# State recurrence of the last attention: how the C rows reach all partitions

## The chip, the cores and the metric

The kernel runs on 1 core of a Trainium2 chip. The metric is the device time of one execution, in microseconds (us), as the median of several runs. Its engines are TensorE (PE in the profile, its weight loads PEld), VectorE (DVE), ScalarE (ACT), GpSimd (POOL) and SyncE (SP), which here only issues DMAs.

## The reference

A decoder of four layers, three sublayers each, on 16 sequences of 128 tokens and 256 features in fp32. What the change touches is the first sublayer of the last layer, a selective state space recurrence (Mamba) with 512 inner channels and 16 states:

```python
dbc = jnp.einsum('bld,ed->ble', x_in, x_proj_w)
delta_in, Bp, Cp = dbc[..., :512], dbc[..., 512:528], dbc[..., 528:]
delta = jax.nn.softplus(jnp.einsum('bld,ed->ble', delta_in, dt_proj_w) + dt_proj_b)
def step(h, inp):
    dt, bt, ct, xt = inp
    dA = jnp.exp(dt[:, :, None] * A[None])
    h = dA * h + dt[:, :, None] * bt[:, None, :] * xt[:, :, None]
    y = jnp.einsum('bds,bs->bd', h, ct) + D * xt
    return (h, y)
```

For each of 16 states there is a value of B and one of C for every token, and each multiplies all 512 channels.

## The kernel before, in words

The last attention is `l3_attn`. Tokens lie along the free dimension, channels on the partitions. The 16 sequences go in 4 groups of 4, so a tile is 128 channels x 512 tokens, and a group has 4 such channel tiles. A **unit** is one state of one pair of channel tiles: 32 units a group (`UNITS`; states 0 to 15 for the first pair of tiles, then again for the second), 128 in all, counted by `n`. A unit goes through the engines in this order:

- TensorE `spread_b` (L2749) spreads row `s` of B over the 128 partitions: a matmul of a 96-row one-hot column with the three bf16 parts of B and C (`bc`). It runs two units ahead in two PSUM banks, and waits until DVE has used the row of two units before.
- DVE (L3013) multiplies it by step times input into a slot of `ring`; ScalarE `decay` (L2912) makes exp(step x A) of both tiles in PSUM; DVE runs two scans (L3019).
- GpSimd (L3097) multiplies the state by the **C row** `s` in `c_row`, a tile of 16 rows that all partitions hold in SBUF.
- TensorE `add_up` (L2766) adds the product to the sums of the two tiles in PSUM, by an fp32 matmul with the identity (four matmul records a unit).

After each half group (16 units) `gate_sums` on DVE (L2996) takes the sums out of PSUM; at unit 1 of a group it takes those of the last half of the group before, and so waits for the last `add_up` of it.

**How C rows come about before the change.** `spread_c` on TensorE spreads a row of C like one of B, into one of two side banks, and `take_c` on ScalarE (L2886) copies it from there to `c_row`. There are 64 of each: 6 before the loop (`EARLY_C`), then one beside unit `n` where `c_row_of(n)` says so: units 0 to 9 of group 0, units 18 to 31 of groups 0 to 2 (rows 0 to 13 of the next group), and units 0 and 1 of groups 1 to 3 (rows 14 and 15).

**What sets the order.** Each engine has one written-out order. In step `n` TensorE does `spread_b(n + 2)`, `spread_c`, `add_up(n - 1)`, then `beside(n)`, the side work of the other groups (projections, convolution L2717, turning L2744). The C rows and the side work share the two side banks in turn:

```python
n = number[name] = len(number)
if n >= 2:
    pe.wait_ge(taken, n - 1)
return net.banks[SIDE[n % 2]]
```

So whatever asks for a side bank waits until ScalarE has emptied it of the work two before. ScalarE does in step `n` `decay(n)`, then, at unit 1 of a group, `silu_z` (L2899) and `silu_u` (L2895), each with a load of its function table, then `take_side(n - 3)` and `take_c` of row `n - 2`; then comes `decay(n + 1)`, with another table load after a silu. `logarithm` (L2891) and `root` (L2903) come at units 18 and 21.

The three bf16 parts of B and C are made once a group: `take_bc` on ScalarE copies the projection from PSUM to `bc` and, in fp32, to `bc_rest[0]` (L2846, L2847); GpSimd `rest` (L3077) subtracts, twice, the second time over `bc_rest[0]`; ScalarE `middle_part` and `low_part` (L2851 to L2857) round. Only then may rows be spread. SP's block is `prefetch`, one DMA of the next sublayer's inputs.

Of the kernel before, what the change touches and what calls it, by code (L numbers as in the profile page):

```python
# [5 lines left out]
F32 = mybir.dt.float32  # L6
# [7 lines left out]
P = 128  # L14
# [2566 lines left out]
    return None  # L2581


EARLY_C = 6


def c_row_of(u):


    g, n = divmod(u, UNITS)  # L2590
    if g == 0 and n + EARLY_C < STATES:
        return 0, n + EARLY_C
    if n >= 18 and g + 1 < GROUPS:
        return g + 1, n - 18
    if n < 2 and g >= 1:
        return g, STATES - 2 + n
    return None


class StepWeights:  # L2600


# [33 lines left out]
def l3_attn(net, prefetch):  # L2636
# [10 lines left out]
    with ExitStack() as sub:  # L2647
# [20 lines left out]
        (filled, taken, part_ready, rest_ready, a_ready, tables_ready, u_ready, z_ready,  # L2668
         bc_ready, ex_ready, lost_ready, positive_ready, log_ready, dt_ready, dtu_ready, b_in_psum, drive_ready,
         decay_ready, state_ready, out_ready, summed, y_taken, yz_ready, r_ready, var_ready, rstd_ready, x_ready,  # L2670
         dve_steps, act_steps) = net.signals(29)
        number = {}
        rows_ = 2 * STATES

# [11 lines left out]
        def normalise(engine, wait, g, b):  # L2686
            wait(rstd_ready, g + 1)
            engine.tensor_scalar(x_of(g)[:, b, :], net.r[:, b, :], net.mv[:, b, 0:1], net.rstd[:, b:b + 1],
                                 ALU.subtract, ALU.mult).then_inc(x_ready, 1)

        with nc.Block() as block:
            @block.sync
            def _(sp):
                prefetch(sp)

            @block.tensor
            def _(pe):
                pe.wait_ge(net.ready["l3_attn"], 16)
# [50 lines left out]
                    return pe.matmul(out[:], pick[:, col:col + 1].broadcast_to([PARTS, P]), bc[g % 2][:],  # L2749
                                     start=True, stop=True)  # L2750

                def spread_c(g, s):
                    spread_out(side("c", g, s), g, STATES + s).then_inc(filled, 1)

                def spread_b(n):
                    if n >= 2:
                        pe.wait_ge(drive_ready, n - 1)
# [36 lines left out]
                for m in range(DT_):  # L2794
                    step_project(0, m)
                pe.wait_ge(tables_ready, 1)
                for s in range(EARLY_C):
                    spread_c(0, s)
                for n in range(2):
                    spread_b(n)  # L2800
                for m in range(DT_):
# [1 line left out]
                for n in range(total):  # L2803
                    if n + 2 < total:
                        spread_b(n + 2)
                    if c_row_of(n):
                        spread_c(*c_row_of(n))
                    if n:
                        add_up(n - 1)
                    beside(n)  # L2810
# [7 lines left out]
            def _(act):  # L2818
# [3 lines left out]
                def bank(*name):  # L2822
                    n = number[name]
                    act.wait_ge(filled, n + 1)
                    return net.banks[SIDE[n % 2]]
# [54 lines left out]
                def take_turned(g, f):  # L2880
                    nc.scalar.copy(net.xT_all[:, g, f, :], bank("turn", g, f)[:]).then_inc(taken, 1)

                def take_c(g, s):
                    if g:
                        act.wait_ge(out_ready, (g - 1) * UNITS + STATES + s + 1)
                    nc.scalar.copy(c_row[:, s, :], bank("c", g, s)[:]).then_inc(taken, 1)  # L2886

                def logarithm(g):
                    act.wait_ge(ex_ready, DT_ * (g + 1))
                    act.wait_ge(lost_ready, DT_ * (g + 1))  # L2890
# [55 lines left out]
                low_part(0)  # L2946
                take_step(0, 2)
                take_step(0, 3)
                for s in range(EARLY_C):
                    take_c(0, s)  # L2950
                logarithm(0)
                act.wait_ge(a_ready, 1)
                act.wait_ge(tables_ready, 1)
                for n in range(total):
                    g, at = divmod(n, UNITS)
                    decay(n)
                    if n < 2:
                        take_conv(1, 2 * n)
                        take_conv(1, 2 * n + 1)
                    if at == 1:  # L2960
                        if g >= 1:
                            silu_z(g - 1)
                        if g + 1 < GROUPS:
                            silu_u(g + 1)
                    if n >= 3:
                        take_side(n - 3)
                    if n >= 2 and c_row_of(n - 2):
                        take_c(*c_row_of(n - 2))
                    if at == 9 and g + 1 < GROUPS:
                        middle_part(g + 1)  # L2970
                    if at == 12 and g + 1 < GROUPS:
                        low_part(g + 1)
                    if at == 18 and g + 1 < GROUPS:
                        logarithm(g + 1)
                    if at == 21 and g >= 1:
                        root(g - 1)
                    if n == total - 2:
                        silu_z(GROUPS - 1)
# [66 lines left out]
            @block.gpsimd  # L3045
            def _(pool):
                tt = nc.gpsimd.tensor_tensor

                def lost_part(g, m):

                    pool.wait_ge(ex_ready, DT_ * g + m + 1)
                    tt(one_ex[m % 2], one_ex[m % 2], ex[:, m, :], ALU.subtract).then_inc(lost_ready, 1)

                def positive_part(g, m):
                    pool.wait_ge(lost_ready, DT_ * g + m + 1)
                    tt(positive[:, m, :], positive[:, m, :], one_ex[m % 2], ALU.subtract).then_inc(positive_ready, 1)

                def step(g, m):
                    pool.wait_ge(log_ready, g + 1)
                    pool.wait_ge(positive_ready, DT_ * g + m + 1)  # L3060
                    if g:
                        pool.wait_ge(decay_ready, 2 * ((g - 1) * UNITS + STATES * (m // 2 + 1)))
                    tt(dt[:, m, :], ex[:, m, :], positive[:, m, :], ALU.add).then_inc(dt_ready, 1)

                def step_times_input(g, m):
                    pool.wait_ge(dt_ready, DT_ * g + m + 1)
                    if g:
                        pool.wait_ge(drive_ready, (g - 1) * UNITS + STATES * (m // 2 + 1))
                    tt(dtu[:, m, :], dt[:, m, :], u[g % 3][:, m, :], ALU.mult).then_inc(dtu_ready, 1)  # L3069

                def rest(g, k):

                    pool.wait_ge(taken, number["bc", g, 0] + 1)
                    pool.wait_ge(part_ready, 2 * g + k + 1)
                    if k:
                        pool.wait_ge(rest_ready, 2 * g + 1)
                    tt(bc_rest[1 - k], bc_rest[k], bc[g % 2][0:rows_, :] if k == 0 else part[:],  # L3077
                       ALU.subtract).then_inc(rest_ready, 1)

                def residual(g, i):  # L3080
                    pool.wait_ge(taken, number["y", g, i] + 1)
                    tt(net.r[:, 2 * i:2 * i + 2, :], net.r[:, 2 * i:2 * i + 2, :],
                       x_of(g)[:, 2 * i:2 * i + 2, :], ALU.add).then_inc(r_ready, 1)

                for m in range(DT_):
                    if m < 2:
                        rest(0, m)
                    lost_part(0, m)
                    positive_part(0, m)
                for m in range(2):  # L3090
                    step(0, m)
                    step_times_input(0, m)
                for n in range(total):
                    g, at = divmod(n, UNITS)
                    pool.wait_ge(state_ready, 2 * n + 2)
                    pool.wait_ge(taken, number["c", g, n % STATES] + 1)
                    tt(ring[n % 4][:], ring[n % 4][:],  # L3097
                       c_row[:, n % STATES, :].unsqueeze(1).broadcast_to([P, 2, T]), ALU.mult).then_inc(out_ready, 1)
                    if at < 2:
                        step(g, 2 + at)  # L3100
                    elif at < 4:
                        step_times_input(g, at)
                    elif at < 8 and g >= 1:
                        gate_by_z(nc.gpsimd, pool.wait_ge, g - 1, at - 4)
                    if g + 1 < GROUPS:
                        if at in (7, 11):
                            rest(g + 1, (at - 7) // 4)
                        if 8 <= at < 16 and at % 2 == 0:
                            lost_part(g + 1, (at - 8) // 2)
                        if 8 <= at < 16 and at % 2 == 1:  # L3110
                            positive_part(g + 1, (at - 9) // 2)
                        if at in (20, 21):
                            step(g + 1, at - 20)
                        if at in (22, 23):
                            step_times_input(g + 1, at - 22)
                    if at in (16, 17) and g >= 1:
                        residual(g - 1, at - 16)
                    if 24 <= at < 28 and g >= 1:
                        normalise(nc.gpsimd, pool.wait_ge, g - 1, at - 24)
                for i in range(2):  # L3120
                    residual(GROUPS - 1, i)
    net.end_sublayer()


# [303 lines left out]
def decoder(nc, x, ctx, out, params, cols, consts):  # L3428
    with ExitStack() as cx:
# [19 lines left out]

        between = [nc.dram_tensor(f"stream{i}", x.shape, F32).ap() for i in range(2)]  # L3450
        net.wkv = nc.dram_tensor("context_quotients", [GROUPS, P, FT * T], F32).ap()
        net.slots_dram = nc.dram_tensor("expert_slots", [EXPERTS * ROWS + SPARE_ROWS, D], F32).ap()
        ctx_g = ctx.rearrange("(g b) t d -> g t b d", b=NB)
        x_g = x.rearrange("(g b) t d -> g t b d", b=NB)
# [320 lines left out]
```

## Time and profile before

| | |
|---|---|
| median of 3 runs | 3082.37 us (3081.39 to 3088.18) |
| the profiled execution's own time, and its span | 3083.43 us, 3081.4 us |
| busy over the span: PE, PEld, DVE, ACT, POOL | 76%, 51%, 50%, 31%, 26% |
| mean granted TensorE clock | 0.877 of full |
| `l3_attn` begins, first unit on DVE, last product on GpSimd | 2126.2, 2193.1, 2713.5 us |
| DMA traffic in slices 29 to 35 of 40 (2157 to 2696 us) | 0 to 1 GB/s |

The shares are means over twelve sublayers with different limits, so they say little of this one. Times in the rows below are us from the start of the span. A timeline row is start, length, engine, line, operation, output<-inputs, shapes, count, and in brackets the idle time before it with what ended it. A row of groups ends in busy us, mean ns of one | idle us before them <- what ended that idle time. Records of TensorE's matmuls overlap, since they are pipelined: in a run of them each takes what the next is later by.

### The profile page before, as it was taken

How to read it: one execution, taken by the hardware profiler on the slowest of the kernel's cores; microseconds unless marked ns; L12 is line 12 of the kernel's file. 1: busy time of each engine (PE TensorE's matmuls, PEld its weight loads, DVE VectorE, ACT ScalarE, POOL GpSimd, SP SyncE). 2: the span in 40 equal slices, each digit the busy share in tenths (PEclk: the TensorE clock that was granted, in tenths of full speed). 3: DMA queues.
4: the chain of work that ended last, by engine and by line, in shares of the span. 5: the costliest groups of instructions: out<-in, count | busy, mean ns of one | idle time of the engine just before them, and what ended most of it. 6: DMA issues, size and time to landing. Idle time of an engine off the chain costs nothing. (4 is left out here: it accounts for less than half of the span.)

```text
span 3081.4 us, 37715 instructions
## 1 busy us (share of the span) xinstructions
PE 2354.0 (76%) x14385; PEld 1558.3 (51%) x14430; DVE 1542.7 (50%) x2929; ACT 964.5 (31%) x1455; POOL 802.6 (26%) x596
## 2 busy tenths in 40 slices
PE   6878759862991882996568877984899896767998
PEld 5655535552881761885335663662344342344554
DVE  3665844441224643002663443233488889945454
ACT  3323313310110331221223320121766665423241
POOL 1121311214003002002001014012578788721221
PEclk9989969976995975998679978996999999978999
DMA  4115010004653003553000011461000000010000
GB/s 138 63 52 199 22 45 1 1 11 143 213 171 115 17 7 143 176 183 109 24 1 22 2 50 67 128 199 36 0 1 1 0 0 1 0 38 7 8 8 14
DMA packets 94449, 186.32 MB, mean 60 GB/s; under 512 B 7744, under 2 KB 78656, under 8 KB 88384
## 3 DMA queue, kind: packets, MB, share of 16 engines
q1 hardware_dynamic: 86592, 162.93, 15.6%
q0 software_dynamic: 7680, 20.98, 2.1%
q8 instruction: 117, 1.92, 0.3%
q14 instruction: 60, 0.49, 0.1%
HBM read 126.22 MB, written 57.67 MB: 60 GB/s over the span
## 5 line engine op out<-in xcount | busy, mean ns | idle before, releaser
L3097 POOL TENSOR_TENSOR l_attn_ring<-l_attn_ring,l_attn_c_rows 128x1024 f32<-128x1024 f32 x128 | 301.2, 2353 | 116.6 <-DVE l_attn_ring L3019 116.1
L3019 DVE TENSOR_TENSOR_SCAN l_attn_ring<-bank,l_attn_ring 128x512 f32<-128x512 f32 x256 | 299.2, 1210 | 17.7 <-ACT bank L2912 13.6
L2766 PE MATMUL bank<-l_attn_ring,identity 128*128 128x512 f32 x512 | 259.9, 632 | 34.4 <-POOL l_attn_ring L3097 30.2
L160 PE MATMUL bank<-x_features,weights 128*128 128x512 f32 x544 | 256.8, 617 | 18.0 <-issue 7.6
L2912 ACT ACTIVATE bank<-l_attn_step,l_attn_minus_exp_a_log 128x508 f32<-128x508 f32 x256 | 174.0, 685 | 183.3 <-DVE l_attn_ring L3019 182.5
L3013 DVE TENSOR_TENSOR l_attn_ring<-l_attn_step_times_input,bank 128x1024 f32<-128x1024 f32 x128 | 154.0, 1203 | 90.6 <-POOL l_attn_step_times_input L3069 66.1
L160 PEld LDWEIGHTS bank<-x_features,weights 128*128 128x128 f32 x544 | 106.3, 198 | 149.7 <-issue 141.9
L2766 PEld LDWEIGHTS bank<-l_attn_ring,identity 128*128 128x128 f32 x512 | 99.3, 200 | 136.4 <-issue 84.7
L3264 PE MATMUL bank<-l_ffn_hidden_parts,l_ffn_sign_weights 128*128 128x512 bf16 x752 | 165.1, 379 | 0.8
L453 DVE TENSOR_REDUCE negmax_slots<-bank 128x16 f32<-128x2048 f32 x48 | 109.8, 2288 | 100.1 <-PE bank L345 99.6
L160 PE MATMUL bank<-l_ffn_tile_xT,l_ffn_tile_weights 128*128 128x256 f32 x664 | 151.6, 383 | 0.8 <-DVE l_ffn_tile_xT L1485 0.4
L169 PE MATMUL bank<-l_ffn_tile_weights,l_ffn_hidden 128*128 128x256 f32 x664 | 149.3, 379 | 0.0
L1350 POOL DMA_INDIRECT l_ffn_tile_weights<-expert_slots,l_ffn_slot_number x48 | 46.7, 973 | 389.5 <-DMA expert_slots<-l_ffn_tile_y 375.4
L169 PE MATMUL bank<-weights,x_features 128*128 128x256 f32 (+2 forms) x448 | 132.0, 450 | 12.4 <-PEq L122 10.6
L160 PEld LDWEIGHTS bank<-l_ffn_tile_xT,l_ffn_tile_weights 128*128 128x128 f32 x664 | 127.3, 192 | 19.5 <-issue 1.3
L169 PEld LDWEIGHTS bank<-l_ffn_tile_weights,l_ffn_hidden 128*128 128x128 f32 x664 | 123.5, 190 | 15.4
L1343 POOL DMA_INDIRECT expert_slots<-x_tokens,l_ffn_slot_number x48 | 46.5, 968 | 286.6 <-DVE l_ffn_slot_number L1441 203.0
L3264 PEld LDWEIGHTS bank<-l_ffn_hidden_parts,l_ffn_sign_weights 128*128 128x128 bf16 x768 | 75.1, 98 | 90.0
L169 PEld LDWEIGHTS bank<-weights,x_features 128*128 128x128 f32 x448 | 94.7, 249 | 46.6 <-issue 36.7
L1416 ACT ACTIVATE l_ffn_hidden<-bank,l_ffn_tile_weights 128x256 f32<-128x256 f32 x120 | 50.3, 470 | 204.5 <-PE bank L160 204.5
L151 PE MATMUL bank<-identity,x_tokens 128*128 128x128 f32 x160 | 34.7, 377 | 100.4 <-DVE x_tokens L199 90.8
L2749 PE MATMUL bank<-l_attn_b_and_c_parts,l_attn_pick_row 96*128 96x512 bf16 x192 | 70.7, 411 | 45.1 <-ACT l_attn_c_rows L2886 15.4
(567 smaller groups left out, 4391.0 us busy)
## 6 DMA issues: line engine op xcount, KB each, us to landing
l_ffn_tile_weights<-l_ffn_experts SPq DMA_DIRECT2D x15, 2180.0 KB, 9.0
ffn_experts_tile_weights<-l_ffn_experts_experts SPq DMA_DIRECT2D x23, 1024.0 KB, 5.8
expert_slots<-zeros SPq DMA_DIRECT2D x8, 2048.0 KB, 13.5
l_ffn_tile_weights<-l_ffn_experts SPq DMA_DIRECT2D x23, 512.0 KB, 4.3
l_ffn_tile_x<-expert_slots SPq DMA_DIRECT2D x38, 256.0 KB, 2.7
expert_slots<-l_ffn_tile_y SPq DMA_DIRECT2D x38, 256.0 KB, 4.9
expert_slots<-zeros SPq DMA_DIRECT2D x1, 5888.0 KB, 27.9
l_ffn_experts_tile_x<-expert_slots SPq DMA_DIRECT2D x23, 256.0 KB, 2.7
```

Of the source, the lines that this page charges most:

```text
L160: mm = pe.matmul(out, w[:, f, m * P:(m + 1) * P], src[:, f, :], start=start and f == 0, stop=stop and f == k - 1)
L169: mm = pe.matmul(out, srcT[:, f, seq(b)], w[:, f, :], start=start and f == 0, stop=stop and f == k - 1)
L453: nc.vector.reduce_max(net.negmax[k % 2][:, :, SHIFT_ROW].rearrange("p (t r) -> p r t", t=4), self.scores.rearrange("p r (t k) -> p r t k" ...
L1350: nc.gpsimd.indirect_dma_start(self.rows[k][:, b, :], None, net.slots_dram, bass.IndirectOffsetOnAxis(ap=self.slot_no[k][:, b:b + 1], axis ...
L1416: ins = net.nc.scalar.activation(self.hidden[t % 2][:, m, :], bank[:, (m % 2) * TILE:(m % 2 + 1) * TILE], self.func, bias=self.b1(t, m))
L2749: return pe.matmul(out[:], pick[:, col:col + 1].broadcast_to([PARTS, P]), bc[g % 2][:], start=True, stop=True)
L2766: mm = pe.matmul(net.banks[SUMS[j]][:], net.ident[:], ring[n % 4][:, j, :], start=s == 0, stop=s == STATES - 1)
L2912: nc.scalar.activation(by_seq(net.banks[DECAY[j]][:])[:, :, 1:], by_seq(dt[:, m, :])[:, :, 1:], ACT.Exp, scale=a[:, m * STATES + s:m * STA ...
L3013: tt(ring[n % 4][:], dtu[:, 2 * half_:2 * half_ + 2, :], net.banks[B_ROW[n % 2]][:].unsqueeze(1).broadcast_to([P, 2, T]), ALU.mult).then_i ...
L3019: nc.vector.tensor_tensor_scan(ring[n % 4][:, j, :], net.banks[DECAY[j]][:], ring[n % 4][:, j, :], 0.0, ALU.mult, ALU.add).then_inc(state_ ...
L3097: tt(ring[n % 4][:], ring[n % 4][:], c_row[:, n % STATES, :].unsqueeze(1).broadcast_to([P, 2, T]), ALU.mult).then_inc(out_ready, 1)
L3264: mm = pe.matmul(bank(m)[:], w1[:, k, m * P:(m + 1) * P], part[:, k, :], start=k == 0 and i == 0, stop=k == 7 and i == 2)
```

## The change

The C rows no longer pass TensorE, PSUM and ScalarE. `EARLY_C`, `c_row_of`, `spread_c` and `take_c` go, and C no longer takes part in the turns of the side banks. After `take_bc` of a group SP stores the 16 rows of C, in fp32, from `bc_rest[0]` to DRAM, waits for it, and then loads row after row back, each by one DMA whose source is the row repeated for 128 partitions. In groups 1 to 3 a load waits until GpSimd is done with the row it replaces (unit 16 + s of the group before); at most 9 loads are under way. GpSimd waits for the loads instead of ScalarE's copies, and its second `rest` waits for the store.

```diff
-EARLY_C = 6
-def c_row_of(u):
...
-         dve_steps, act_steps) = net.signals(29)
+         dve_steps, act_steps, c_stored, *c_loaded) = net.signals(38)
+        C_SIGNALS = len(c_loaded)
...
+        def wait_c(engine, n):
+            engine.wait_ge(c_loaded[n % C_SIGNALS], 16 * (n // C_SIGNALS + 1))
...
-                def spread_c(g, s):
-                    spread_out(side("c", g, s), g, STATES + s).then_inc(filled, 1)
...
                 pe.wait_ge(tables_ready, 1)
-                for s in range(EARLY_C):
-                    spread_c(0, s)
...
                         spread_b(n + 2)
-                    if c_row_of(n):
-                        spread_c(*c_row_of(n))
...
-                def take_c(g, s):
-                    if g:
-                        act.wait_ge(out_ready, (g - 1) * UNITS + STATES + s + 1)
-                    nc.scalar.copy(c_row[:, s, :], bank("c", g, s)[:]).then_inc(taken, 1)
...
-                for s in range(EARLY_C):
-                    take_c(0, s)
...
-                    if n >= 2 and c_row_of(n - 2):
-                        take_c(*c_row_of(n - 2))
...
                     if k:
                         pool.wait_ge(rest_ready, 2 * g + 1)
+                        pool.wait_ge(c_stored, 16 * (g + 1))
...
-                    pool.wait_ge(taken, number["c", g, n % STATES] + 1)
+                    if n % UNITS < STATES:
+                        wait_c(pool, g * STATES + n % STATES)
...
+            @block.sync
+            def _(sp):
+                prefetch(sp)
+                for g in range(GROUPS):
+                    sp.wait_ge(taken, number["bc", g, 0] + 1)
+                    sp.dma_start(net.c_rows[g], bc_rest[0][STATES:rows_, :]).then_inc(c_stored, 16)
+                    sp.wait_ge(c_stored, 16 * (g + 1))
+                    for s in range(STATES):
+                        n = g * STATES + s
+                        if g:
+                            sp.wait_ge(out_ready, (g - 1) * UNITS + STATES + s + 1)
+                        if n >= C_SIGNALS:
+                            wait_c(sp, n - C_SIGNALS)
+                        sp.dma_start(c_row[:, s, :], net.c_rows[g][s:s + 1, :].broadcast_to([P, T])).then_inc(
+                            c_loaded[n % C_SIGNALS], 16)
...
+        net.c_rows = nc.dram_tensor("state_outputs", [GROUPS, STATES, T], F32).ap()
```

## Rows read from the trace of the kernel before

**Rows 1.** Groups of instructions on DVE, 2190 to 2722 us.
```profile
L3019 DVE TENSOR_TENSOR_SCAN l_attn_ring<-bank,l_attn_ring 128x512 f32<-128x512 f32 x256 | 299.2, 1210 | 17.7 <-ACT bank L2912 13.6
L3013 DVE TENSOR_TENSOR l_attn_ring<-l_attn_step_times_input,bank 128x1024 f32<-128x1024 f32 x128 | 154.0, 1203 | 90.6 <-POOL l_attn_step_times_input L3069 66.1 <-PE bank L2749 24.0
L2996 DVE SCALAR_TENSOR_TENSOR l_attn_conv_silu<-l_attn_conv_silu,weights,bank 128x512 f32<-128x512 f32 x16 | 11.2, 743 | 21.7 <-PE bank L2766 21.7
```
**Rows 2.** Timeline of two free units in group 2, DVE.
```profile
2568.97 1.20 DVE L3013 TENSOR_TENSOR l_attn_ring<-l_attn_step_times_input,bank 128x1024 f32<-128x1024 f32 x1
...
2572.45 1.20 DVE L3013 TENSOR_TENSOR l_attn_ring<-l_attn_step_times_input,bank 128x1024 f32<-128x1024 f32 x1
```
**Rows 3.** Groups of instructions on PE, same stretch: B and C rows together.
```profile
L2749 PE MATMUL bank<-l_attn_b_and_c_parts,l_attn_pick_row 96*128 96x512 bf16 x184 | 66.7, 404 | 40.2 <-ACT l_attn_c_rows L2886 13.5 <-ACT x_features L2881 11.6 <-DVE l_attn_ring L3013 10.4
```
**Rows 4.** Groups of instructions on ACT, same stretch.
```profile
L2912 ACT ACTIVATE bank<-l_attn_step,l_attn_minus_exp_a_log 128x508 f32<-128x508 f32 x256 | 174.0, 685 | 183.3 <-DVE l_attn_ring L3019 182.5 <-POOL l_attn_step L3063 0.5
L2886 ACT COPY l_attn_c_rows<-bank 128x512 f32<-128x512 f32 x58 | 33.5, 577 | 0.3 <-PE bank L2749 0.3
```
**Rows 5.** Timeline, before the first unit.
```profile
2181.04 1.26 POOL L3052 TENSOR_TENSOR weights<-weights,l_attn_exp_minus_abs 128x512 f32<-128x512 f32 x1 [0.53 <-ACT weights L2872]
...
2184.51 1.28 ACT L2891 ACT_TABLE_LOAD   x1
...
2193.10 7.03 PE L2717 MATMUL bank<-weights 128*128 128x512 f32 x16 [0.92 <-ACT l_attn_conv_silu L2836]
```
**Rows 6.** Windows: length, busy of PE, PEld, DVE, ACT, POOL, PEclk, DMA, GB/s.
```profile
2202.90:2207.20 4.30, 0.34 (x2) 0.00 (x0) 1.02 (x1) 4.26 (x5) 0.98 (x1) 0.91 0.00 0
2207.20:2211.00 3.80, 3.75 (x5) 1.48 (x6) 3.77 (x5) 1.91 (x4) 2.41 (x2) 0.50 0.01 2
```
**Rows 7.** Timeline, unit 7 of group 0.
```profile
2224.74 1.22 DVE L3013 TENSOR_TENSOR l_attn_ring<-l_attn_step_times_input,bank 128x1024 f32<-128x1024 f32 x1 [2.29 <-PE bank L2749]
```
**Rows 8.** Timeline of group 0 from unit 20 (first row) to 31 (last).
```profile
2274.97 1.20 DVE L3013 TENSOR_TENSOR l_attn_ring<-l_attn_step_times_input,bank 128x1024 f32<-128x1024 f32 x1
...
2283.02 0.60 PE L2749 MATMUL bank<-l_attn_b_and_c_parts,l_attn_pick_row 96*128 96x512 bf16 x2
...
2283.46 1.88 PE L2766 MATMUL bank<-l_attn_ring,identity 128*128 128x512 f32 x4
...
2285.17 3.56 PE L2717 MATMUL bank<-weights 128*128 128x512 f32 x8
...
2319.07 1.20 DVE L3013 TENSOR_TENSOR l_attn_ring<-l_attn_step_times_input,bank 128x1024 f32<-128x1024 f32 x1
```
**Rows 9.** Timeline of group 1, units 20 and 31 on DVE.
```profile
2408.70 1.20 DVE L3013 TENSOR_TENSOR l_attn_ring<-l_attn_step_times_input,bank 128x1024 f32<-128x1024 f32 x1
...
2453.57 1.20 DVE L3013 TENSOR_TENSOR l_attn_ring<-l_attn_step_times_input,bank 128x1024 f32<-128x1024 f32 x1
```
**Rows 10.** Timeline, start of group 2.
```profile
2466.33 0.56 ACT L2881 COPY x_features<-bank 128x512 f32<-128x512 f32 x1
...
2466.79 0.59 ACT L2886 COPY l_attn_c_rows<-bank 128x512 f32<-128x512 f32 x1
...
2466.95 0.61 PE L2749 MATMUL bank<-l_attn_b_and_c_parts,l_attn_pick_row 96*128 96x512 bf16 x1 [6.14 <-ACT x_features L2881]
...
2471.01 1.41 DVE L2996 SCALAR_TENSOR_TENSOR l_attn_conv_silu<-l_attn_conv_silu,weights,bank 128x512 f32<-128x512 f32 x2 [6.91 <-PE bank L2766]
```
**Rows 11.** Timeline, start of group 3.
```profile
2597.35 0.57 ACT L2881 COPY x_features<-bank 128x512 f32<-128x512 f32 x1
...
2601.10 1.41 DVE L2996 SCALAR_TENSOR_TENSOR l_attn_conv_silu<-l_attn_conv_silu,weights,bank 128x512 f32<-128x512 f32 x2 [4.18 <-PE bank L2766]
```
**Rows 12.** Timeline, B and C of group 0 kept in fp32, and overwritten.
```profile
2161.68 0.57 ACT L2847 COPY ctx_tokens<-bank 32x512 f32<-32x512 f32 x1
...
2172.14 1.15 POOL L3077 TENSOR_TENSOR ctx_tokens<-ctx_tokens,l_attn_b_and_c_part 32x512 f32<-32x512 f32 x1
```
**Rows 13.** DMA issues: count, KB each, median us to landing.
```profile
expert_slots<-l_ffn_experts_tile_y SPq DMA_DIRECT2D x23, 256.0 KB, 5.6
```

More of the change, by code:

```diff
@@ L2581, in side_work @@
     return None
-EARLY_C = 6
-def c_row_of(u):
[L2590 to L2597, printed above, removed]
 class StepWeights:
@@ L2689, in normalise @@
                                  ALU.subtract, ALU.mult).then_inc(x_ready, 1)
+        def wait_c(engine, n):
+            engine.wait_ge(c_loaded[n % C_SIGNALS], 16 * (n // C_SIGNALS + 1))
         with nc.Block() as block:
-            @block.sync
-            def _(sp):
-                prefetch(sp)
             @block.tensor
```

## The prediction, made before the changed kernel ran

> **What bounds the kernel now.** Only one sublayer of twelve is touched, so the page's shares decide nothing. I read the groups of instructions of that stretch first, then the timeline unit by unit, then windows for TensorE's clock.
>
> On VectorE the groups [rows 1] add up to the recurrence: 256 scans of 1.21 us and 128 products of 1.20 us. Where nothing holds a unit up, products start 3.48 us apart [rows 2] (the scans overlap by a little). 128 x 3.48 = 445 us, while VectorE's first product starts at 2193.1 and GpSimd's last, some 5 us behind VectorE, at 2713.5 (table above): about 515 us for the same work and some 18 us of sums and statistics. VectorE sets the pace; what a change here can win is its idle time. [Rows 1] names it: 24.0 us for B rows from TensorE, 21.7 for sums from TensorE, 13.6 for the decay from ScalarE (the 66.1 lies before the first unit). So nearly 60 us are lost, three quarters of them to TensorE being late.
>
> TensorE is late for two reasons. It is full where side work runs. And it waits in order: [rows 3] has 13.5 us of idle time ended by a C copy and 11.6 by a copy of turned features, the latter before a spread row, and a B row asks for no side bank, so it is the C row that waits. ScalarE itself has room: its decays wait 182.5 us for the scans [rows 4].
>
> **The change part by part.** Removed are 64 spreading matmuls and 64 copies of 0.58 us, 58 of each inside the recurrence. The copies are 33.5 us of ScalarE [rows 4], but that engine mostly waits, so they count only where a decay is late. The matmul in a run costs what the next is later by: B and C together last 0.60, one alone ends in 0.38, so 0.22 us at the full clock. The removed sums alone, 58 x 0.22 = 13 us, are not the answer; place by place:
>
> - *Before the first unit.* The 6 early copies delay the logarithm's table load to 2184.51, while GpSimd's last lost part, which it also waits for, ends at 2181.04 + 1.26 = 2182.30 [rows 5]. Without them everything up to the first unit is about 2.15 us earlier. But the third unit waits for a chain that goes through 16 convolution matmuls (7.03 us at 0.44 each, [rows 5]). They start when ScalarE has taken the first results, in unit 0. Now TensorE had 0.92 us idle before them; after the change its earlier work is done some 7 us before. [Rows 6] shows such a case: after a window of 4.3 us with 0.34 us of work the granted clock is 0.50, the lower level of 1.2 GHz. At that level each costs 0.44 us more; 4 to 8 of them cold cost 1.8 to 3.5 us, which eats the 2.15. I take 0, between 2.15 gained and 1.3 lost.
>  The Trainium skill's page on TensorE (TensorE: Matmul & The Clock Gate, HAM oscillation) says that idle gaps bring the clock down and the next batch starts cold, thus work taken off a waiting TensorE can be paid back; the trace agrees (0.50). A reader who let the clock alone would book the 2.15 as a gain.
> - *Group 0, units 3 to 10.* A C row a unit, with projections. VectorE waits 2.29 us for a B row at unit 7 [rows 7]. TensorE has one cold stretch there by waiting for a C copy; it will still be idle then, for unit 3 is late. With the side work in front of that B row starting up to 1 to 2 us earlier I take 1.2, between 0 and 2.4.
> - *Group 0, units 20 to 31.* C rows in each, convolutions in every second. A pair of units needs of TensorE 2 x (0.44 for B and C + 1.71 for sums, 4 at 0.43) + 3.4 (8 at 0.43) = 7.7 us [rows 8]; VectorE needs 2 x 3.48 = 6.97. TensorE binds. Without C the pair needs 7.27, still over 6.97, but TensorE also starts this stretch earlier, because the C row of step 18 waits for ScalarE behind the logarithm, with the sums and a projection behind it. By following its order from there, each B row comes in time up to unit 27 or so, and the deficit of 0.3 a pair eats only that lead. From unit 20 to 31 it now takes 2319.07 - 2274.97 = 44.1 us; free it is 11 x 3.48 = 38.3. With 0.1 to 0.3 of rest: 5.6 gained. If the lead is not there, it is 3 x 0.43 + some, about 3.
> - *Group 1, units 20 to 31.* 2453.57 - 2408.70 = 44.9 us [rows 9] against 38.3 + 0.3, since `root` with its two table loads makes the decay of unit 22 late even then: 6.2. Group 2 has no projections here and nearly no stall; 0.3.
> - *Start of group 2.* The dearest stall. The C row of step 64 needs the side bank of the turned features, whose copy stands on ScalarE behind two silus and ends at 2466.89 [rows 10]. TensorE idles 6.14 us, and the last sums of group 1, ready long before, are queued behind; cold they come late, and VectorE waits 6.91. Without the C row the sums are done before VectorE asks at 2471.01 - 6.91 = 2464.1. What is late next is the decay of unit 2: turned copy until 2466.89, no C copy, table load 1.28, one exp 0.69, so the scan starts at 2468.9; now it starts at 2471.01 + 1.41 + 1.25 - 0.09 = 2473.6. Gained 4.7; I take 4.6.
> - *Start of group 3.* The same with one silu less: turned copy until 2597.9 [rows 11], + 1.28 + 0.69 = 2599.9. Free of the 4.18 VectorE would begin the sums at 2601.10 - 4.18 = 2596.9 and the scan 1.41 + 1.25 - 0.09 later, at 2599.5, so it waits 0.4: 3.7 gained. Start of group 1: there the sums are in time and only the C copy before the table load goes, 0.6.
> - *Added: SP's DMAs.* 4 stores of 32 KB, 64 loads of 256 KB = 16.8 MB, on a queue that does nothing else and DMA engines that are idle there. The store of group 0 can start at 2161.68 + 0.57 = 2162.25; the subtraction that now waits for it starts at 2172.14 [rows 12], 9.9 us of cover. The nearest row, 256 KB stores, lands in 5.6 us [rows 13]: hidden, from 0 to that. The first C row is needed at about 2194.6, the 16th at about 2258; loads from 2168 on, so up to (2258 - 2168) / 16 = 5.6 us a row is hidden. In later groups a row is free in unit 16 + s and wanted in unit 32 + s: the last of 16 may come 31 units, 110 us, after the first is free, 6.9 us a row. I cost it at nothing: even one at a time, rows of the dearest kind of 256 KB [rows 13] would just do, and 9 may be under way. If that cover were gone, GpSimd, and behind it `add_up` and the ring, would wait for all of it.
>
> Sum: 0 + 1.2 + 5.6 + 0.6 + 6.2 + 4.6 + 0.3 + 3.7 = 22.2 us. The profiled execution took 3083.43 (span 3081.4), so 3061.2; the median shown is 1.1 lower: 3060.
>
> **The rivals.**
> 1. *The relief is half given back.* The two stretches with convolutions stay bound by TensorE (7.27 against 6.97) with no lead, or more TensorE idling brings more cold matmuls, as [rows 6] has it. For: the pair's sum. Against: the waits for C that set it back are gone too. The stretches then give 5 instead of 11.8, the first units 0, the start loses 1.3: 22.2 - 6.8 - 1.2 - 1.3 = 12.9 gained, 3069.5.
> 2. *The start's gain stays*, if the convolutions run warm, and the first units give 2.4: 22.2 + 2.2 + 1.2 = 25.6, 3057.
> 3. *Slower: the row loads are slow.* 128 reads of the same 2 KB of DRAM; no row of this trace has such a load. It decides from 5.6 us a row in group 0 and 6.9 later. At 8 us the last row of group 0 is 16 x 2.4 = 38 us late, those of the three others 16 x 1.1 = 18 each, 92 less 22 gained: 3152. Against: 16 engines share it, and 256 KB stores need 5.6 us one by one.
>  On that the Trainium skill (DMA: Bandwidth & Descriptors, Rules for kernel authors) says that a leading repeated dimension of fewer than 16 copies confines a DMA to that many engines. Here 128 copies lead, so by the rule it isn't confined; no run shows it yet.
> 4. *Nothing*: the stalls pass to ScalarE's decays, whose 13.6 us [rows 1] would have to grow to 30. Against: 182.5 us of waiting on that engine, and copies of its own that go.
>
> **How the numbers follow.** My forecast has 0.66, rival 1 0.15, rival 2 0.10, rival 3 0.05, rival 4 0.04. The forecast's own range is 3055 to 3067; the range given reaches to rival 1: 3053 to 3070. A measurement can tell 0.2%, 6.2 us: faster is below 3076.2. The first three cases lie there but for a tail of rival 1: 0.89 faster, 0.05 same, 0.06 slower.
>
> **What would show it.** VectorE's idle time before L2996 falls from 21.7 to about 10 or less, that ended by TensorE's B rows from 24.0 to under 12; the sum of waits for decays stays or rises by some us. Units 20 to 31 of groups 0 and 1 take some 38.5 us. Unit 2 of group 2 has its scan wait for the decay. GpSimd waits for no DMA. Wrong it would be if products of free units were over 3.48 us apart (the DMAs would then slow the engines), if GpSimd waited for loads, or if units 20 to 31 of group 0 stayed over 43 us.

## The result, and the profile after

The kernel with the change took 3063.0 us (3059.43 to 3068.74, 5 runs) beside 3085.13 us (3081.39 to 3089.1, 5 runs) before: ratio 0.9927, 95% interval 0.9914 to 0.994. The forecast was a gain of 22.2 us, to 3060 us; the medians differ by 22.1. By the interval the gain lies between 18.5 and 26.5 us, so the nearness of the two figures is luck.

The profiled executions took 3083.43 and 3060.37 us. The sublayer began 1.55 us earlier in the second (SP's first issue in it, 2124.62 for 2126.17), which the change can't cause. Nearly all the rest lies in it: from that issue to the start of GpSimd's last product, called the **stretch** from here on, 587.3 us before and 565.9 after, 21.4 less.

The groups of instructions on DVE, 2186 to 2700 us, of the kernel after:

```profile
L2988 DVE TENSOR_TENSOR_SCAN l_attn_ring<-bank,l_attn_ring 128x512 f32<-128x512 f32 x256 | 299.1, 1210 | 20.2 <-ACT bank L2885 16.2
L2982 DVE TENSOR_TENSOR l_attn_ring<-l_attn_step_times_input,bank 128x1024 f32<-128x1024 f32 x128 | 153.6, 1200 | 79.0 <-POOL l_attn_step_times_input L3038 63.4 <-PE bank L2734 15.1
L2965 DVE SCALAR_TENSOR_TENSOR l_attn_conv_silu<-l_attn_conv_silu,weights,bank 128x512 f32<-128x512 f32 x16 | 11.1, 737 | 8.9 <-PE bank L2748 8.9
```

The work is the same as in [rows 1]; the waits aren't. Those for sums fell from 21.7 to 8.9 us, those for B rows from 24.0 to 15.1 (I had said under 12), those for decays rose from 13.6 to 16.2. TensorE's own group, same stretch:

```profile
L2734 PE MATMUL bank<-l_attn_b_and_c_parts,l_attn_pick_row 96*128 96x512 bf16 x126 | 49.4, 394 | 18.0 <-DVE l_attn_ring L2982 17.2
```

Against [rows 3], no wait for ScalarE is left in it: what holds these matmuls up is now VectorE's use of the B rows. And what GpSimd and SP show of the new path, in the answers for the tile of C rows and for the store:

```profile
L3068 POOL TENSOR_TENSOR l_attn_ring<-l_attn_ring,l_attn_c_rows x128: 2338/2352/2387, 2192.5 to 2690.5; 128x1024 f32<-128x1024 f32 x128
L3107 SPq DMA_DIRECT2D l_attn_c_rows<-state_outputs x64: 319/320/608, 2161.8 to 2573.1; - x64
...
  DVE l_attn_ring L2988: 97.6, 58
...
DMA to landing us min/median/max: 3.0/3.2/6.6
```

The only wait of GpSimd's products is for VectorE; a row lands in 3.2 us (median of all 64). The 16 of group 0, issued in 9.61 us with up to 9 under way, have a median of 5.4 us and at most 6.6; the 48 later ones 3.1.

To see where the time went I cut the stretch at the starts of VectorE's products (group.unit), from the timelines:

| us | before | after | gained | forecast |
|---|---|---|---|---|
| SP's issue to 0.0 | 66.92 | 64.25 | 2.67 | |
| 0.0 to 0.2 | 7.30 | 9.63 | -2.33 | sum of both 0 |
| 0.2 to 0.20 | 74.59 | 74.00 | 0.59 | 1.2 |
| 0.20 to 0.31 | 44.10 | 38.84 | 5.26 | 5.6 |
| 0.31 to 1.3 | 17.68 | 17.21 | 0.47 | 0.6 |
| 1.3 to 1.20 | 71.94 | 71.95 | 0 | 0 |
| 1.20 to 1.31 | 44.87 | 38.60 | 6.27 | 6.2 |
| 1.31 to 2.3 | 22.27 | 17.68 | 4.59 | 4.6 |
| 2.3 to 2.31 | 110.55 | 110.26 | 0.29 | 0.3 |
| 2.31 to 3.3 | 19.54 | 15.88 | 3.66 | 3.7 |
| 3.3 to GpSimd's last | 107.59 | 107.59 | 0 | 0 |

The start of group 2 after the change, timeline; the lines answer to [rows 10]:

```profile
2449.55 1.38 DVE L2965 SCALAR_TENSOR_TENSOR l_attn_conv_silu<-l_attn_conv_silu,weights,bank 128x512 f32<-128x512 f32 x2
...
2451.08 3.75 PE L2748 MATMUL bank<-l_attn_ring,identity 128*128 128x512 f32 x4 [3.37 <-DVE l_attn_conv_silu L2965]
2451.86 0.57 ACT L2859 COPY x_features<-bank 128x512 f32<-128x512 f32 x1
...
2452.45 1.28 ACT L2885 ACT_TABLE_LOAD   x1
...
2454.53 2.34 DVE L2988 TENSOR_TENSOR_SCAN l_attn_ring<-bank,l_attn_ring 128x512 f32<-128x512 f32 x2 [2.47 <-ACT bank L2885]
```

VectorE takes the sums with no wait, where it waited 6.91 us. The wait moved, smaller, to the decay: after the turned copy (2451.86) come the table load and the exp, and the scan waits 2.47.

The place before the third unit, where the gain of the start was given back (timeline, then a window with busy of PE, PEld, DVE, ACT, POOL, and the clock):

```profile
2188.89 9.35 PE L2702 MATMUL bank<-weights 128*128 128x512 f32 x16 [7.80 <-ACT l_attn_conv_silu L2814]
...
2198.50 1.22 DVE L2982 TENSOR_TENSOR l_attn_ring<-l_attn_step_times_input,bank 128x1024 f32<-128x1024 f32 x1 [2.55 <-PE bank L2734]
```
```profile
2189.00:2193.00 4.00, 4.00 (x5) 1.71 (x6) 3.97 (x4) 1.45 (x3) 0.46 (x1) 0.50 0.00 0
```

After 7.80 us idle the same 16 matmuls take 9.35 us for the 7.03 of [rows 5], at the lower clock level (0.50, 1.2 GHz) in the window shown, and the third product waits 2.55 us behind them.

One part of the table is not the change's. The sublayer starts with 16 projection matmuls, ahead of everything that was edited:

```profile
2124.67 9.12 PE L160 MATMUL bank<-x_features,weights 128*128 128x512 f32 x16 [1.67 <-PEq L122]
```

They took 9.64 us in the profile before, and over the twelve profiles of this document between 8.74 and 10.12. Without them the time to 0.0 is 57.27 to 57.28 us in the two kernels that spread the early C rows, and 55.13 to 55.15 in the ten others: 2.15 us less, the rest of the 2.67 is these matmuls. So of the 21.4 us some 20.9 are the change's.

### The profile page after: what moved, and what is told of

Its sections match the earlier page's. It is cut to its first block and busy times, and to the rows that moved or that the text cites. A ratio compares the mean times of both kernels' runs of the same rounds, so it can differ in the third digit from the quotient of the medians.

```text
span 3058.3 us, 37468 instructions
## 1 busy us (share of the span) xinstructions
PE 2336.4 (76%) x14321; PEld 1552.2 (51%) x14366; DVE 1540.7 (50%) x2929; ACT 932.2 (30%) x1391; POOL 801.8 (26%) x596
## 5 line engine op out<-in xcount | busy, mean ns | idle before, releaser
L2988 DVE TENSOR_TENSOR_SCAN l_attn_ring<-bank,l_attn_ring 128x512 f32<-128x512 f32 x256 | 299.1, 1210 | 20.2 <-ACT bank L2885 16.2
L1485 DVE COPY l_ffn_tile_xT<-bank 128x512 f32<-128x512 f32 x38 | 26.2, 691 | 156.3 <-PE bank L1372 156.3
```

The source lines that it names most:

```text
L2988: nc.vector.tensor_tensor_scan(ring[n % 4][:, j, :], net.banks[DECAY[j]][:], ring[n % 4][:, j, :], 0.0, ALU.mult, ALU.add).then_inc(state_ ...
```

## The experiments

All are built on the kernel after, or mix both. Each ran beside the kernel before on the same chip; the absolute times of chips differ, so ratios and the stretch are compared. Theory: the gain is TensorE's waits in order, at the places of the table.

**Rows 14 and 15 of groups 1 to 3 by DMA, the others spread.**

```diff
+def by_dma(row):
+    g, s = row
+    return g >= 1 and s >= STATES - 2
```

> The kernel before, but rows 14 and 15 of groups 1 to 3 (6 of the 64, those spread beside units 0 and 1 of a group) come by DMA; all others are still spread and copied. Measure: the stretch from SP's first issue in this sublayer to the start of GpSimd's last product, 587.3 us before (2126.17 to 2713.5) and 565.9 after (2124.62 to 2690.5). Theory (the order at the group starts: a C row waits for the bank of the turned features and holds up the last sums): group 2's start gives back 4.6 less one C copy, 4.0, group 3's 3.1, group 1's nothing: 580.2 us. Rival (each row costs its share, 21.4 / 64): 585.3 us.

Measured: ratio 0.9987 (0.9977 to 0.9997), stretch 582.8, between the two forecasts. Cut as in the table, the two places are as the theory had them: 1.31 to 2.3 took 18.17 us (4.1 gained, 4.0 said), 2.31 to 3.3 16.37 (3.2, 3.1 said). But 1.3 to 1.20 took 73.41 us for 71.95, and 1.20 to 1.31 46.04 for 44.87, where the edit changes nothing. At both places TensorE's clock was lower than in the kernel before. Ahead of unit 7, where 1.36 of the first is lost, four matmuls for the sums took 3.44 us at a granted clock of 0.53 (the last experiment shows such a place in full). Ahead of unit 21, where 1.04 of the second is lost, the granted clock was 0.50 over 4.8 us; in the kernel before it was 1.00 and then 0.56 there. Why it fell just there stays open.

**The complement: those six rows spread, the others by DMA.**

```diff
+    return g == 0 or s < STATES - 2
```

> The complement: rows 14 and 15 of groups 1 to 3 are still spread and copied beside units 0 and 1, all others come by DMA. Theory, refined: it is not a C row at the group's start that hurts, but its place in the turns of the side banks. With rows 12 and 13 gone, row 14 needs the bank of the first turned tile, which is empty in time, so the sums pass; only row 15, behind them, waits. So the gain stays but for a C copy and some cold matmuls: 566 to 568 us. Rival A (any C row there blocks the sums): 565.9 + 7.1 to 8.7 = 573 to 575 us. Rival B (share): 567.9 with the loss spread over all units, not at the group starts.

Measured: ratio 0.9932 (0.9907 to 0.9957), stretch 566.4, with 17.68 and 15.89 at the two starts, those of the kernel after. In its timeline the last sums pass, and the C row behind them takes the wait:

```profile
2420.10 1.38 DVE L3010 SCALAR_TENSOR_TENSOR l_attn_conv_silu<-l_attn_conv_silu,weights,bank 128x512 f32<-128x512 f32 x2
...
2423.03 0.61 PE L2761 MATMUL bank<-l_attn_b_and_c_parts,l_attn_pick_row 96*128 96x512 bf16 x1 [4.77 <-ACT x_features L2894]
```

So the dearest stall comes not from rows that are spread at a group's start, but from where they fall in the turns of two banks. Either edit frees the sums at the two starts (7.3 us gained there by six rows, 8.2 by the other 58 of the 64), so these gains neither add up nor go by the number of rows.

**TensorE's time back, without bank turns and copies.**

```diff
+                    if twice:
+                        spread_out(net.banks[B_ROW[n % 2]], n // UNITS, n % STATES)
```

> The kernel after, but beside each of the 58 units that had a C row TensorE spreads the B row twice into the same bank: its time of a C matmul without bank turns and without a copy. Theory (most of the gain came from waits in order, and TensorE has a lead in the convolution stretches): the deficit of a pair of units goes from 0.3 back to 0.73 us and eats the lead; group 0 loses about 2, group 1 about 0.7, the first units 0.5 to 1: 569.4 us, 568.5 to 571. Rival (TensorE's own time is the gain, 58 x 0.22 = 12.8 us): 578.7 us.

Measured: ratio 0.9948 (0.993 to 0.9966), stretch 571.0. Cut: 0.20 to 0.31 1.9 us more (2 said), 1.20 to 1.31 0.9 more (0.7 said), 0.2 to 0.20 0.8 more (0.5 to 1 said); the other 1.4 of the 5.1 lie before the third unit. Of these, 0.8 is the first 16 projections (9.93 us for 9.12), 0.4 the 16 cold matmuls before the third unit (9.75 for 9.35), and 0.2 the third unit's own doubled B row. So 58 spreads of 0.22 us are worth some 3.8 us, not 12.8.

**ScalarE's time back.**

```diff
+                    if n >= 2 and c_row_of(n - 2):
+                        chain.settle()
+                        chain.step(nc.scalar.copy(unused, net.xT_all[64:P, GROUPS - 1, 1, :]))
```

> The kernel after, but ScalarE makes a copy of 64 x 512 in SBUF, used by nobody, at each of the 58 places where it copied a C row. Theory (ScalarE's time counts only where a decay is late: one copy ahead of the table load at each of three group starts, and some units of group 0 with the long step chain): 2 to 4 us more, 568.9 us. Rival (ScalarE's time is the gain): 33.5 us more, 599 us, or a good part of it.

Measured: ratio 0.9961 (0.9945 to 0.9977), stretch 573.0, so 7.1 us more for 2 to 4 said. 0.9, 0.65 and 0.65 us of it are at the three group starts, 0.8 in 1.20 to 1.31, 1.1 in 0.2 to 0.20, 2.1 in 2.3 to 2.31 (1.55 of these at one unit, see below), 1.0 before the third unit, ahead of the first copy (0.7 of it the first 16 projections, 0.3 the 16 cold matmuls). VectorE's waits for decays:

```profile
L3008 DVE TENSOR_TENSOR_SCAN l_attn_ring<-bank,l_attn_ring 128x512 f32<-128x512 f32 x256 | 299.2, 1210 | 24.4 <-ACT bank L2902 20.5
```

20.5 us for 16.2. Without the 1.55 and the 1.0, some 4.5 us are ScalarE's, more than I gave it and far from 33.5. Its copies were dearer in the kernel after than I had worked out from their places.

**TensorE kept at work before the first unit.**

```diff
-                for n in range(2):
-                    spread_b(n)
-                for m in range(DT_):
+                spread_b(0)
+                for m in range(2):
                     convolve(1, m)
+                for _ in range(30):
+                    spread_out(net.banks[B_ROW[1]], 0, 1)
+                spread_b(1)
+                for m in range(2, DT_):
+                    convolve(1, m)
```

> The kernel after, but TensorE spreads one B row 30 times (6.4 us) in the 7.8 us in which it idles before the third convolution of group 1; the last spread is the one that is used. Theory (the start's 2.15 us were eaten by the lower clock after that idle time): the 16 convolution matmuls take 7.0 us, not 9.35, and the third unit begins 2.3 us earlier relative to the first: stretch 563.6 us, 563.2 to 564. Rival (the third unit waits for something else): 565.9 us, and the wait before its product stays 2.5 us.

Measured: stretch 564.1, just outside the 563.2 to 564 (its first projections took 9.85 us for 9.12); ratio 0.9932 (0.9914 to 0.995). From 0.0 to 0.2 7.30 us instead of 9.63, and the wait for the B row is gone but for 0.23:

```profile
2163.75 1.22 DVE L2986 TENSOR_TENSOR l_attn_ring<-l_attn_step_times_input,bank 128x1024 f32<-128x1024 f32 x1 [0.23 <-PE bank L2734]
```

The 16 matmuls still wait for the same result of ScalarE and start 0.02 us after 0.0 in both kernels; but the granted clock over the 4 us after 2156.0 is 1.00, and they take 7.03 us for 9.35. That shows the cause of the give-back. To see whether it pays, it ran again beside the kernel after:

> The kernel after, unchanged, on the chip of the next two: it shows how far the stretch of one kernel moves from profile to profile. Theory (what moves it is where TensorE's lower clock falls, as the profiles so far suggest): 565.9 us within 2 us either way, the steps at the group starts the same within 0.3 us. Rival (the differences of 2 to 3 us between the experiments outside their edits come from the edits): within 0.5 us of 565.9.

> The kernel with TensorE kept at work before the first unit (30 spreads of an unused row), beside the kernel after on one chip. Theory: from the first product on VectorE to the third 7.3 us against 9.6, and a stretch 2 us shorter than that of the kernel after in the same call; in the medians 2 us of 3050, below what the rounds tell apart. Rival (the extra work is paid back by the clock or elsewhere): no shorter stretch.

Measured: the kernel after 3059.1 us, stretch 565.6, which both forecasts allow, so this repetition alone decides nothing; ratio 0.9929 (0.9916 to 0.9943); with the spreads 3061.0 us, stretch 564.5, 0.9934 (0.9919 to 0.9948). The 2.3 us from 0.0 to 0.2 are there again (7.30 for 9.53, and in this trace the 16 matmuls take 7.03 us), but 0.0 came 1.2 us later than in its neighbour. All of that is the first 16 projections, before anything that was edited:

```profile
2123.46 10.12 PE L160 MATMUL bank<-x_features,weights 128*128 128x512 f32 x16 [1.68 <-PEq L122]
```
```profile
2121.99 8.92 PE L160 MATMUL bank<-x_features,weights 128*128 128x512 f32 x16 [1.67 <-PEq L122]
```

From 4 to 6 us after SP's issue the granted clock was 0.50 in the first of these, 1.00 in the second. Without them the stretch is 2.2 us shorter, as forecast, and nothing was paid back elsewhere; but the medians don't tell the two kernels apart, and it is not shown to beat the change in the time of an execution. The cuts of the kernel after came back within 0.01 us from 0.20 on. Over the kernels that don't touch the place, the 16 cold matmuls before the third unit moved too, between 9.16 and 9.80 us.

**One load under way.**

```diff
-        C_SIGNALS = len(c_loaded)
+        C_SIGNALS = 1
```

> The kernel after, but one row load under way instead of 9: about 3.2 + 0.3 = 3.5 us a row. Theory (hidden up to 5.6 us a row in group 0 and 6.9 later): 565.9 us, no wait of GpSimd for a DMA. Rival (the depth of 9 is what hides them): GpSimd waits for rows, more than 2 us more.

Measured: ratio 0.9926 (0.9902 to 0.9951), stretch 567.5. The 1.6 us over the kernel after lie before 0.20, 0.9 of them in the first projections (10.02 us) and 0.45 in the 16 cold matmuls (9.80), which the edit doesn't touch. No wait of GpSimd for a DMA. The depth of 9 is not needed.

**And every row loaded twice.**

```diff
+                        sp.dma_start(c_row[:, s, :], net.c_rows[g][s:s + 1, :].broadcast_to([P, T])).then_inc(again, 16)
+                        sp.wait_ge(again, 16 * (n + 1))
```

> As the one before, and every row is loaded twice, the second load after the first has landed: about 7 us a row. Theory (the cover is 5.6 us a row in group 0): the 16th row of group 0 lands at about 2162 + 16 x 7 = 2274 us, wanted at about 2255: 19 us late, and 0 to 3 us late in each later group: stretch 585 to 594 us. Rival (the cover is wider than I worked out): under 570 us.

Measured: ratio 0.9993 (0.998 to 1.0006), stretch 583.9: nearly the whole gain is gone, a little less than I had said (585 to 594), but not by the wait that I had named. The rows come every 6.0 us, and GpSimd waits for two of them, 2.2 us in all. The rest is here (timelines of POOL and of SP's queue):

```profile
2227.79 1.14 POOL L3048 TENSOR_TENSOR ctx_tokens<-ctx_tokens,l_attn_b_and_c_part 32x512 f32<-32x512 f32 x1 [18.65 <-DMA state_outputs<-ctx_tokens]
```
```profile
2224.26 0.32 SPq L3110 DMA_DIRECT2D l_attn_c_rows<-state_outputs  x1
2224.62 0.43 SPq L3100 DMA_DIRECT2D state_outputs<-ctx_tokens  x1
```

SP issues the store of group 1 only behind the 16th row of group 0, and the second subtraction of group 1 waits for it. GpSimd was free for it at 2209.1; rows began at 2127.3; the subtraction began 3.2 us after the store's issue; so by my estimate the cover is (2209.1 - 3.2 - 2127.3) / 16 = 4.9 us a row, tighter than the 5.6 I gave.

**The store issued by GpSimd.**

```diff
-                    sp.dma_start(net.c_rows[g], bc_rest[0][STATES:rows_, :]).then_inc(c_stored, 16)
+                    if k == 0:
+                        pool.dma_start(net.c_rows[g], bc_rest[0][STATES:rows_, :]).then_inc(c_stored, 16)
```

> As the kernel with two loads a row (6.0 us a row), but GpSimd issues the store, ahead of its first subtraction, so that it doesn't stand behind 16 row loads in SP's queue. Theory (the 18.65 us in which GpSimd waited for the store of group 1 came from that queue, and the rows themselves cost only the 2.2 us seen): stretch 566 to 571 us, GpSimd's wait for the store under 1 us, for rows some 2 to 6 us. Rival (slow row loads cost it either way): about 584 us, with the waits before the products with C rows.

Measured: ratio 0.9945 (0.9926 to 0.9964), stretch 572.1, 1.1 above the range that was said. The 18.65 us are gone, and the rows, now the only thing late, cost GpSimd 10.4 us of waits in 6 places, more than the 2 to 6 said:

```profile
  DVE l_attn_ring L2989: 91.4, 54
  DMA l_attn_c_rows<-state_outputs: 10.4, 6
```

Of the 6.2 us over the kernel after, 4.3 are in 0.2 to 0.20. And 1.6 are in 2.3 to 2.31, where nothing was edited; there the four matmuls for the sums ran cold (3.56 us for 1.98), and the projection behind them, 3.62 us in both kernels, started late. The trace of this kernel (timeline and window), then the same place of the kernel after:

```profile
2460.43 3.56 PE L2749 MATMUL bank<-l_attn_ring,identity 128*128 128x512 f32 x4 [0.92 <-POOL l_attn_ring L3071]
...
2460.30:2463.70 3.40, 3.27 (x4) 1.18 (x4) 3.37 (x4) 1.38 (x2) 3.40 (x3) 0.51 0.20 77
...
2473.28 1.22 DVE L2983 TENSOR_TENSOR l_attn_ring<-l_attn_step_times_input,bank 128x1024 f32<-128x1024 f32 x1 [1.39 <-PE bank L2735]
```
```profile
2459.35 1.98 PE L2748 MATMUL bank<-l_attn_ring,identity 128*128 128x512 f32 x4 [0.93 <-POOL l_attn_ring L3068]
...
2461.00:2464.40 3.40, 3.40 (x9) 0.80 (x8) 3.37 (x4) 1.29 (x3) 3.40 (x3) 1.00 0.00 0
```

The same unit, number 7 of a group, was late by as much in the first experiment (1.4 us, group 1) and in that with the copies (1.55, group 2). In both the four matmuls for the sums were slow too, 3.44 and 3.02 us, at a granted clock of 0.53 and 0.50. So it is the lower clock in all three; what made it fall in these kernels and not in the others isn't shown.

## Why the prediction was right

**The sum.** 22.2 us was forecast for the profiled execution; 21.4 came inside the sublayer, 20.9 without the first projections. The profiled executions differ by 23.1, since 1.55 more came before the sublayer. Four terms, the two stretches with convolutions and the starts of groups 2 and 3, are 19.8 of it (20.1 said), each within 0.35 us.

**The method that carried it.** It wasn't the busy time removed (two experiments put TensorE's at some 3.8 and ScalarE's at some 4.5 us, each alone), but asking at each stall which instruction TensorE stood before, and what was queued behind it. Even if the two simply add up, which no run shows, the matmul and copy times leave over half of the gain. For some 6 us of it (the 7.3 of the first experiment less 1.3 for the copies), at the starts of groups 2 and 3, the first two experiments show that it lies in the turns of the side banks. In the convolution stretches each experiment gave back only a part (2.9 and 0.8 of 11.5 us); that the rest lies in those turns too fits [rows 3] and the forecast, but no run put back the turns there alone.

**The start.** Right, and for the reason given: 2.15 us earlier by the change, as forecast, and 2.3 paid back by the clock, where I had taken a loss of 1.8 to 3.5. The granted clock was 0.50 after 7.80 us of idle time, and with the gap filled the matmuls took 7.03 us. The rule of the Trainium skill weighed there (TensorE: Matmul & The Clock Gate, HAM oscillation), that such gaps bring the clock down, agrees with both. The other 0.5 of the 2.7 in the table is the first projections (16 matmuls in 9.12 us for 9.64), which have nothing to do with the change.

**Group 0, units 3 to 10.** The mis-sized term: 0.6 for 1.2. TensorE idled 4.02 us there before the change, waiting for a C copy; after it, 5.46 us, waiting for VectorE's product of unit 3, and the four matmuls for the sums behind it were cold in both (3.62 and 3.78 us). The step to unit 6 became 0.4 us longer, those to units 7, 9 and 13 0.4 to 0.5 shorter. That the idle time in another place is what held the term down is my reading; no run takes it out alone.

**The indicator for B rows** was wrong (15.1, said under 12): 2.55 of the 15.1 are the third unit's wait, which my own term for the start implies and which I left out of the indicator.

**The DMAs.** At nothing, rightly: a store lands in 1.6 us, a row in 3.2 (medians), and the stretch of free units from 1.3 to 1.20 took 71.95 us before and after. But the bound on them was wrong in kind. I worked out when rows are wanted and forgot that the next group's store stands behind them in SP's queue, with GpSimd's subtraction, and through it all B rows, waiting. Rival 3, slow loads, would have decided from about 5 us a row, by that wait. Rivals 1, 2 and 4 didn't come: the convolutions had the lead, the clock was cold, and ScalarE's decays took only 2.6 us more.

## What to carry to other kernels

Where two kinds of work share a small ring of buffers in a written-out order, price a removed item by the wait that it stands in and by what is queued behind it, not by its own time; the same item can cost 0.2 us in one place and 4.6 in another. When work is moved to a queue, go through that queue in order and ask of each transfer what stands ahead of it, above all of a small store that another engine waits for. And work taken off TensorE ahead of a dependent batch may come back as that batch's lower clock.

## What the runs showed that I had not expected

A load of 2 KB of DRAM repeated to 128 partitions (256 KB) lands in 3.0 us alone, beside 2.8 us (median) for the plain 256 KB loads of the same profile (`l_ffn_tile_x<-expert_slots`); reading one place 128 times costs at most 0.2 us more. With up to 9 under way each takes 5.4 us (median), but one is issued every 0.6 us. And from 0.20 on the cuts of the same work repeat within 0.03 us from profile to profile, but for one place. What moves a profile, apart from that, is where TensorE's lower clock falls: up to 1.4 us in the first projections, up to 0.6 in the matmuls before the third unit, and 1.4 to 1.6 at unit 7 of a group, in three of the twelve.
